# Latent attention and two window layers on one core: guard, turns from x, weight loads, paired values

## The chip, the cores and the metric

One NeuronCore of a Trainium2 chip runs the whole program. The metric is device time in microseconds (us), the median of the runs of one kernel. The engines are TensorE (PE; its weight loads PEld), VectorE (DVE), ScalarE (ACT), GpSimd (POOL) and SyncE (SP), which here only issues transfers. Each engine works through its own queue in order; semaphores tie them together.

## The reference

x has 4 sequences of 1024 tokens, 128 channels, float32.

```python
x = x + layernorm(latent_attention(layernorm(x)))      # 16 heads of 8, causal softmax over 1024 keys
x = x + layernorm(window_layers(layernorm(x)))         # 2 layers

# a window layer: 8 heads of 64, windows of 64 tokens, each sees itself and the one before
h = shift_token(x)                    # half of the channels from the token before
q, k, v = split(h @ wqkv)
q = q / clip(norm(q), 1e-12) * qs     # k the same
q, k = rotary_xpos(q, k)
x = x + local_attention(q, k, v) @ wo
h = layernorm(shift_token(x)) * lg + lb
a, g = split(h @ w1 + b1)
x = x + (a * gelu(g)) @ w2 + b2
```

## The kernel before, in words

The program is a row of stages; a block of instructions for each engine ends before the next begins. `project` makes the queries, keys and values of the latent attention; `attend` is the causal attention; `mix` multiplies with W_o, normalises and adds; then for each of two layers `window` and `mlp`; `last_norm` closes.

**attend** runs 16 stages (4 sequences x 4 groups of 4 heads). A stage has 12 score groups, called steps here (0 to 11): step n covers one half of the queries (steps 0 to 3 the first half, 4 to 11 the second) and one tile of 128 keys, for 4 heads; the widths are 512, 384, 256, 128 and 512 five times, 384, 256, 128 columns. For each step TensorE issues four scores (L444) into a ring of three banks, psE, and between them four "maxima units" of the next stage (L429, with the causal mask L432) into a ring of four banks, psM. ScalarE takes the exponential of each score (L514) into one of four `prob` buffers; VectorE takes the maximum of each unit (L593); GpSimd masks the diagonal tiles (L549). Behind the scores of step G TensorE issues `values(G - 2)`: four heads side by side as tiles of 128 rows by 32 columns of its array, float32, two passes each (L458, eight instructions), summed in one bank, psO. At a half's end ScalarE copies psO (L526, at steps 2 and 6) and the next first key tile's values wait for it; TensorE turns the copy (L478, behind the scores of steps 4 and 8). Maxima of the next stage are turned as 12-column transposes (L470) behind the scores of steps 0 and 5.

**mix** works on 8 chunks of 512 tokens. ScalarE first copies a chunk of `o_tok` into `oc` (L740), TensorE turns it (L719), ScalarE copies the turn (L736), TensorE multiplies with W_o (L726), then statistics, normalisation and residual go between VectorE, GpSimd and ScalarE.

**window** works on 32 tiles of 128 tokens per layer, in slots: in slot s tile s is projected (L904, L908), tile s-1 normalised, tile s-2 turned and scored, tile s-3 goes through softmax and values, tile s-4 through `wo`. The x of tile s+2 is turned for its projection (L897) near the end of the slot. SyncE first copies it from `xf` to a staging tile `xc` (L875), and spreads the values V of tile t over two buffers `vb` (L881, L882). The order of SyncE's queue is: x of tiles 0 and 1, the 14 loads of the MLP's weights (L660 to L673), then per slot x of tile s and V of tile s-2.

For the norms ScalarE squares, VectorE sums per head (L1135) and guards against zero with a tensor_scalar maximum (L1139), GpSimd raises to -0.5 (L1102, the `pow`). GpSimd's queue per slot is: `pow` of tile s-1, four sine products of tile s, called rotations here (L1092), and their addition to the cosine product (L1097). VectorE's queue per slot is: K copies (L1159, from PSUM, and L1162, within SBUF), reciprocal (L1179) and product (L1182) of the softmax, residual (L1186), cosine product (L1144), two maxima (L1169), carry (L1130), copy (L1174), the product with the norms (L1153, which waits for `pow` and for the addition), sums (L1135), guard (L1139). At a layer's start VectorE clears three tiles, scales the cosine and sine tables and then makes the first carries.

```python
dve.tensor_scalar(ssm[:, r % 2, :], ss[:, r % 2, :], 1e-24, None, ALU.max).then_inc(ssm_done, 1)      # L1139
ge(act, av_done, G - NPROB + 1)                                                                       # ScalarE, before the exponentials of step G
halves(sp, av_done, t, -4)                                                                            # SyncE, before V of tile t is spread
```

## Time and profile before

| | us |
|---|---|
| median of 3 runs | 1540.82 (1539.07 to 1544.87) |
| profiled execution | 1543.41 |
| its span, first to last instruction | 1541.6 |
| attend, first maximum to last score group | 80 to 609 |
| mix | 611 to 656 |
| window layer 1, from its first turn | 661 to 994 |
| window layer 2, from its first turn | 1089 to 1424 |
| last norm | 1515 to 1541.6 |

| engine | busy us | share of the span |
|---|---|---|
| PE | 1299.2 | 84% |
| DVE | 1211.1 | 79% |
| ACT | 946.1 | 61% |
| POOL | 766.6 | 50% |

An engine is busy while one of its instructions runs; an instruction that has begun and waits inside counts as busy. The shares are means over stages with different limits, so the stages are to be read one by one.

### The profile page before, as it was taken

The page shows a single profiled execution, that of the slowest core. Times are in us where ns is not written, and L with a number is a line of the kernel's source. Part 1 is how long each engine was busy: PE and PEld are TensorE (multiplying, and loading weights), DVE is VectorE, ACT ScalarE, POOL GpSimd, SP SyncE. Part 2 cuts the span into 40 slices and gives each one's busy share as a digit, 9 for nine tenths or more (in the row PEclk, how much of TensorE's full clock was granted, in tenths as well). Part 3 has the DMA queues.
Part 4 walks back from the last instruction along what each step waited for, and adds up shares of the span by engine and source line. Part 5 has one row for each costly group of instructions (what it writes and reads, how often), then busy time and mean ns, then how long its engine had stood idle before and what let it go on. Part 6 is the DMA issues. An engine that isn't in the chain of part 4 may idle for free. (4 is left out here: it accounts for less than half of the span.)

```text
span 1541.6 us, 30997 instructions
## 1 busy us (share of the span) xinstructions
PE 1299.2 (84%) x11013; PEld 741.1 (48%) x11013; DVE 1211.1 (79%) x2530; ACT 946.1 (61%) x2605; POOL 766.6 (50%) x742
## 2 busy tenths in 40 slices
PE   4389999999999997359999999699589999997892
PEld 2243444444444442326666666465266666665561
DVE  5576878787888770659999999666499999997667
ACT  4425776777677766747777777332377777775220
POOL 1001212221222121469999999310599999994102
PEclk9757999999999998679999999989799999999896
DMA  4412111111111101121111111000211111110001
GB/s 111 141 47 65 36 51 50 36 34 53 48 36 35 36 4 41 56 50 36 36 36 36 36 36 32 9 1 1 49 27 36 36 36 36 36 34 16 1 1 55
DMA packets 44272, 59.59 MB, mean 39 GB/s; under 512 B 8130, under 2 KB 31948, under 8 KB 41804
## 3 DMA queue, kind: packets, MB, share of 16 engines
q1 hardware_dynamic: 43544, 57.47, 13.8%
q8 instruction: 89, 1.46, 0.4%
q14 instruction: 63, 0.52, 0.1%
q10 hardware_dynamic: 576, 0.15, 0.0%
HBM read 26.67 MB, written 8.39 MB: 23 GB/s over the span
## 5 line engine op out<-in xcount | busy, mean ns | idle before, releaser
L593 DVE TENSOR_REDUCE a_nm<-a_psM 128x1 f32<-128x512 f32 (+3 forms) x768 | 375.1, 550 | 118.2 <-PE a_psM L429 65.8
L514 ACT ACTIVATE a_prob<-a_psE 128x512 f32<-128x512 f32 (+3 forms) x768 | 326.2, 491 | 161.7 <-PE a_psE L444 160.1
L1092 POOL TENSOR_TENSOR w_t<-w_raw,w_sin 128x256 f32<-128x256 f32 x256 | 264.1, 1060 | 49.6 <-ACT w_raw L1018 49.6
L429 PE MATMUL a_psM<-a_ks,a_qs 72*128 72x512 bf16 (+3 forms) x768 | 251.9, 346 | 18.3 <-PEq L76 18.1
L549 POOL TENSOR_SCALAR_AFFINE_SELECT a_prob<-a_prob 128x512 f32<-128x512 f32 x128 | 81.4, 637 | 371.9 <-ACT a_prob L514 371.9
L444 PE MATMUL a_psE<-a_qs,a_ks 84*128 84x512 bf16 (+3 forms) x768 | 253.2, 339 | 9.4 <-DMA a_qs<-a_nmT 5.8
L1041 ACT ACTIVATE w_prob<-w_psS,w_bias 128x128 f32<-128x128 f32 x512 | 181.4, 367 | 48.5 <-DVE w_bias L1169 48.4
L1102 POOL TENSOR_TENSOR w_rn<-w_ssm,mhalf 128x16 f32<-128x16 f32 x64 | 186.5, 2914 | 6.4
L458 PE MATMUL a_psO<-a_prob,v_all 128*32 128x512 f32 (+3 forms) x1536 | 170.1, 510 | 11.5 <-ACT a_oT L526 11.5
L444 PEld LDWEIGHTS a_psE<-a_qs,a_ks 84*128 84x128 bf16 x768 | 74.6, 99 | 188.5 <-ACT a_prob L514 118.2
L1097 POOL TENSOR_TENSOR w_rot<-w_t 128x1024 f32<-128x1024 f32 x64 | 152.1, 2376 | 8.8 <-issue 0.4
L904 PE MATMUL w_psQK<-w_wqkv,w_hT 128*128 128x512 f32 x256 | 132.4, 642 | 0.2 <-ACT w_raw L1018 0.2
L432 PE MATMUL a_psM<-mask_q,ident_b 128*128 128x128 bf16 x512 | 116.6, 229 | 0.0
L1041 ACT ACTIVATION_READ_ACCUMULATOR w_prob<-w_psS,w_bias 128x1 f32 x512 | 104.3, 204 | 0.0
L1048 ACT ACTIVATE w_pT<-w_psT 128x512 f32<-128x512 f32 x64 | 38.2, 597 | 106.8 <-PE w_psT L948 106.8
L429 PEld LDWEIGHTS a_psM<-a_ks,a_qs 72*128 72x128 bf16 x768 | 78.2, 102 | 49.2 <-issue 23.5
L1144 DVE TENSOR_TENSOR w_t<-w_raw,w_cos 128x1024 f32<-128x1024 f32 x64 | 78.0, 1218 | 28.8 <-ACT w_raw L1018 23.9
L1153 DVE TENSOR_TENSOR w_rot<-w_rot,w_rn 128x1024 f32<-128x1024 f32 x64 | 91.3, 1426 | 3.2 <-POOL w_rn L1102 1.5
L1169 DVE TENSOR_REDUCE w_bias<-w_psS 128x4 f32<-128x512 f32 x128 | 87.0, 680 | 3.1 <-PE w_psS L937 3.1
L1277 PE MATMUL f_psU<-f_hT,f_w 128*114 128x512 f32 (+1 forms) x192 | 88.0, 609 | 0.0
L1139 DVE TENSOR_SCALAR w_ssm<-w_ss 128x16 f32<-128x16 f32 x64 | 82.3, 1286 | 2.2
L963 PE MATMUL w_psO<-w_pT,w_vb 128*64 128x64 f32 x1024 | 57.9, 234 | 27.5 <-ACT w_pT L1048 15.5
(139 smaller groups left out, 2509.9 us busy)
## 6 DMA issues: line engine op xcount, KB each, us to landing
w_vb<-w_v SPq DMA_DIRECT2D x128, 128.0 KB, 2.3
a_qs<-q_parts SPq DMA_DIRECT2D x16, 576.0 KB
a_ks<-k_parts SPq DMA_DIRECT2D x16, 576.0 KB
w_xc<-xf_sb SPq DMA_DIRECT2D x64, 64.0 KB, 2.0
q_parts<-p_parts SPq DMA_DIRECT2D x24, 128.0 KB
k_parts<-p_parts SPq DMA_DIRECT2D x24, 128.0 KB
out_x<-l_y SPq DMA_DIRECT2D x8, 256.0 KB, 2.3
a_qs<-a_nmT SPq DMA_DIRECT2D x32, 48.0 KB
```

The source lines that it names most:

```text
L429: mm = pe.matmul(out, qs[0:ROWS, g, j, i * P:(i + 1) * P], ks[0:ROWS, g, j, 512 * kc:512 * kc + n], start=True, stop=not diag)
L432: mm = pe.matmul(out[:, n - P:n], sb["ident_b"], sb["mask_q"], start=False, stop=True)
L444: pe.matmul(psE[:, r % NRING, 0:w], ks[0:KROWS, g, j, kt * P:(kt + 1) * P], qs[0:KROWS, g, j, q0:q0 + w], start=True, stop=True).then_inc( ...
L458: mm = pe.matmul(psO[32 * j:32 * j + 32, q0:512], v_flat[:, col + j * VA:col + j * VA + 32], prob[G % NPROB][:, j, 0:512 - q0], start=(kt ...
L514: act.activation(prob[G % NPROB][:, j, 0:w], psE[:, r % NRING, 0:w], ACT.Exp, scale=SCALE0).then_inc(e_read, 1)
L593: dve.tensor_reduce(nm[:, s % 2, kc, i, j:j + 1], psM[:, r % MRING, 0:n], AX.X, ALU.max, negate=True).then_inc(m_read, 1)
L904: pe.matmul(psQK[:, w, :], hT[:, r % 2, 0:P], wqkv[:, bass.ds(layer * (3 * INNER) + w * INNER, INNER)], start=True, stop=True).then_inc(qk ...
L1041: i = act.activation(prob[:, p, w, c, :], psS[:, w, c * P:(c + 1) * P], ACT.Exp, bias=bias[:, p, n:n + 1], accum_out=den[:, p, n:n + 1])
L1092: i = pool.tensor_tensor(out[:, w, :, half, :], src[:, w, :, 1 - half, :], tab, ALU.mult)
L1097: pool.tensor_tensor(rot[:, r % 2, :], t1[:, :], t2[:, :], ALU.add).then_inc(rot_done, 1)
L1102: pool.tensor_tensor(rn[:, r % 2, :], ssm[:, r % 2, :], sb["mhalf"][:, 0:16], ALU.pow).then_inc(rn_done, 1)
L1153: dve.tensor_tensor(both, both, rn[:, p, :].unsqueeze(2).broadcast_to((P, 16, DH)), ALU.mult).then_inc(unit_done, 1)
```

## The change

Four edits. The guard becomes a reduction with maximum over pairs: `ss` gets a second element beside each sum, set once per layer to 1e-24. In the window layers TensorE turns x straight from `xf`, the copies through `xc` go, and the MLP's weights are loaded behind V of tile 7. In the mix TensorE turns straight from `o_tok`, and ScalarE's copy goes. In attend the values are issued behind the scores of odd steps only, two groups at once, with five `prob` buffers.

```diff
--- before.py
+++ after.py
@@ -367,7 +367,7 @@
         def sem(name):
             return ctx.enter_context(nc.semaphore(name))
 
-        NPROB, NRING, MRING = 4, 3, 4
+        NPROB, NRING, MRING = 5, 3, 4
         qs, ks, v_flat = sb["qs"], sb["ks"], sb["v_flat"]
         prob = [tile(f"a_prob{r}", [P, HG, 512]) for r in range(NPROB)]
         oT = tile("a_oT", [P, 2, 512])
@@ -496,8 +496,10 @@
                     for qc in range(2):
                         if o_turn_group(e, qc) == G:
                             turn_outputs(e, qc)
-                if G >= AV_LAG:
-                    values(G - AV_LAG)
+                if G % 2:
+                    for behind in (AV_LAG + 1, AV_LAG):
+                        if G >= behind:
+                            values(G - behind)
             for G in GROUPS[-AV_LAG:]:
                 values(G)
             turn_outputs(NSTAGE - 1, 1)
@@ -682,7 +684,6 @@
         def sem(name):
             return ctx.enter_context(nc.semaphore("m_" + name))
 
-        oc = tile("m_oc", [P, 2, 4, P])
         ocT = tile("m_ocT", [P, 2, 4, P])
         stats = tile("m_stats", [P, 2, 4, 4, 6])
         mv = tile("m_mv", [P, 2, 4, 4, 2])
@@ -693,7 +694,7 @@
         psT = ctx.enter_context(nc.psum_tensor("m_psT", [P, 2, 512], F32))
         psA = ctx.enter_context(nc.psum_tensor("m_psA", [P, 4, 512], F32))
 
-        w_in, o_staged, oT_done, oT_copied, a_done = sem("w_in"), sem("o_staged"), sem("oT_done"), sem("oT_copied"), sem("a_done")
+        w_in, oT_done, oT_copied, a_done = sem("w_in"), sem("oT_done"), sem("oT_copied"), sem("a_done")
         stats_done = [sem("stats_a"), sem("stats_x")]
         mean_done = [sem("mean_a"), sem("mean_x")]
         var_done = [sem("var_a"), sem("var_x")]
@@ -712,11 +713,10 @@
             pe.wait_ge(w_in, 16)
 
             def turn(c, r):
-                at_least(pe, o_staged, 0, c, 1)
                 at_least(pe, oT_copied, 0, c, -1)
                 p = r % 2
                 for t in range(4):
-                    i = pe.transpose(psT[:, p, t * P:(t + 1) * P], oc[:, p, t, :], sb["ident"])
+                    i = pe.transpose(psT[:, p, t * P:(t + 1) * P], sb["o_tok"][:, c * 4 + t, :], sb["ident"])
                 i.then_inc(oT_done, 1)
 
             def project_out(c, r):
@@ -735,10 +735,6 @@
                 at_least(act, a_done, 0, c, -1)
                 act.activation(ocT[:, r % 2, :, :].rearrange("p t c -> p (t c)"), psT[:, r % 2, :], ACT.Copy).then_inc(oT_copied, 1)
 
-            def stage(c, r):
-                at_least(act, oT_done, 0, c, -1)
-                act.activation(oc[:, r % 2, :, :], sb["o_tok"][:, bass.ts(c, 4), :], ACT.Copy).then_inc(o_staged, 1)
-
             def normal(w, c, p, outs, ins, done):
 
                 at_least(act, shift_done[w], 0, c, 1)
@@ -753,7 +749,7 @@
             def layers_input(c, r):
                 normal(1, c, r, lambda t: sb["xf"][:, c * 4 + t, :], lambda t: sb["x"][:, c * 4 + t, :], xf_done)
 
-            pipelined(act, NCH, 4, [(1, copy), (0, stage), (3, normal_a), (5, layers_input)])
+            pipelined(act, NCH, 4, [(1, copy), (3, normal_a), (5, layers_input)])
 
         @block.gpsimd
         def _(pool):
@@ -823,10 +819,9 @@
 
         wqkv, wo = sb["wqkv"], sb["wo"]
         cos, sin = tile("w_cos", [P, TB, 2, DH]), tile("w_sin", [P, TB, 2, DH])
-        xc = tile("w_xc", [P, 2, D])
         hT = tile("w_hT", [P, 2, P + 1])
         sq = tile("w_sq", [P, 2 * INNER])
-        ss, ssm, rn = tile("w_ss", [P, 2, 16]), tile("w_ssm", [P, 2, 16]), tile("w_rn", [P, 2, 16])
+        ss, ssm, rn = tile("w_ss", [P, 2, 16, 2]), tile("w_ssm", [P, 2, 16]), tile("w_rn", [P, 2, 16])
         raw = tile("w_raw", [P, 2, 2 * INNER])
         t1, t2 = tile("w_t1", [P, 2 * INNER]), tile("w_t2", [P, 2 * INNER])
         rot = tile("w_rot", [P, 2, 2 * INNER])
@@ -845,7 +840,6 @@
         psO = ctx.enter_context(nc.psum_tensor(f"w_psO_{layer}", [P, 512], F32))
 
         w_in, tables, zeroed = sb["w_in"], sem("tables"), sem("zeroed")
-        xc_in = [sem("xc_in0"), sem("xc_in1")]
         vb_in = [sem(f"vb_in{r}") for r in range(4)]
         xT_done, hT_copied, carried = sem("xT_done"), sem("hT_copied"), sem("carried")
         qk_done, v_done, sq_done, ss_done, ssm_done, rn_done = (sem(x) for x in ("qk_done", "v_done", "sq_done", "ss_done", "ssm_done", "rn_done"))
@@ -870,10 +864,6 @@
 
         @block.sync
         def _(sp):
-            def load_x(t, r):
-                at_least(sp, xT_done, base, t, -1)
-                sp.dma_start(xc[:, r % 2, :], sb["xf"][:, t, :]).then_inc(xc_in[r % 2], 16)
-
             def spread_v(t, r):
 
                 at_least(sp, v_copied, base, t, 1)
@@ -881,20 +871,18 @@
                 sp.dma_start(vb[r][0:WIN, :], v[r][0:WIN, :]).then_inc(vb_in[r], 16)
                 sp.dma_start(vb[(r + 1) % 4][WIN:P, :], v[r][WIN:P, :]).then_inc(vb_in[r], 16)
 
-            sp.wait_ge(zeroed, layer * 3 + 3)
-            for t in range(2):
-                load_x(t, t)
-            load_mlp_weights(nc, sp, io, sb, layer)
-            pipelined(sp, NT, 4, [(0, lambda t, r: None if isinstance(t, int) and t < 2 else load_x(t, r)), (2, spread_v)])
+            sp.wait_ge(zeroed, layer * 4 + 4)
+            for t in range(NT):
+                if t == 8:
+                    load_mlp_weights(nc, sp, io, sb, layer)
+                spread_v(t, t % 4)
 
         @block.tensor
         def _(pe):
             def turn_x(t, r):
-                p = r % 2
-                pe.wait_ge(xc_in[p], (base + t - p) * 8 + 16)
                 at_least(pe, pT_copied[0], base, t, -4)
                 at_least(pe, hT_copied, base, t, 0)
-                pe.transpose(psT[:, 0, 0:P], xc[:, p, :], sb["ident"]).then_inc(xT_done, 1)
+                pe.transpose(psT[:, 0, 0:P], sb["xf"][:, t, :], sb["ident"]).then_inc(xT_done, 1)
 
             def project_qk(t, r, w):
                 if w == 0:
@@ -1074,7 +1062,7 @@
                 if runs(s - 2):
                     exps(s - 2, r2, 1)
 
-            act.wait_ge(zeroed, layer * 3 + 3)
+            act.wait_ge(zeroed, layer * 4 + 4)
             copy_hT(0, 0)
             copy_hT(1, 1)
             slots(act, slot)
@@ -1110,6 +1098,7 @@
             dve.memset(hT[WIN:P, 1, P:P + 1], 0.0).then_inc(zeroed, 1)
             dve.memset(kT[:, 1, :, :], 0.0).then_inc(zeroed, 1)
             dve.memset(vb[0][WIN:P, :], 0.0).then_inc(zeroed, 1)
+            dve.memset(ss[:, :, :, 1], 1e-24).then_inc(zeroed, 1)
 
             dve.wait_ge(w_in, WINDOW_LOADS)
             for w in range(2):
@@ -1119,7 +1108,7 @@
                     sc = sb["scales"][:, bass.ds(layer, 1), w, 32 - 32 * half:64 - 32 * half].broadcast_to((P, TB, 32))
                     part = slice(32 * half, 32 * half + 32)
                     dve.tensor_tensor(sin[:, :, w, part], sb["sin"][:, :, w, part], sc, ALU.mult).then_inc(tables, 1)
-            dve.wait_ge(zeroed, layer * 3 + 3)
+            dve.wait_ge(zeroed, layer * 4 + 4)
             dve.wait_ge(tables, layer * 6 + 6)
 
             def carry(t, r):
@@ -1132,11 +1121,11 @@
 
             def sums(t, r):
                 at_least(dve, sq_done, base, t, 1)
-                dve.tensor_reduce(ss[:, r % 2, :], sq[:, :].rearrange("p (h d) -> p h d", d=DH), AX.X, ALU.add).then_inc(ss_done, 1)
+                dve.tensor_reduce(ss[:, r % 2, :, 0], sq[:, :].rearrange("p (h d) -> p h d", d=DH), AX.X, ALU.add).then_inc(ss_done, 1)
                 at_least(dve, ss_done, base, t, 1)
                 at_least(dve, rn_done, base, t, -1)
 
-                dve.tensor_scalar(ssm[:, r % 2, :], ss[:, r % 2, :], 1e-24, None, ALU.max).then_inc(ssm_done, 1)
+                dve.tensor_reduce(ssm[:, r % 2, :], ss[:, r % 2, :, :], AX.X, ALU.max).then_inc(ssm_done, 1)
 
             def cosines(t, r):
                 at_least(dve, raw_done, base, t, 1)
```

## Rows read from the trace of the kernel before

**Rows 1.** Stretches: us, busy PE, PEld, DVE, ACT, POOL (count), PE clock, DMA share, GB/s.
```profile
240.00:340.00 100.00, 97.44 (x798) 44.20 (x800) 80.06 (x174) 71.83 (x174) 22.19 (x51) 1.00 0.14 40
700.00:800.00 100.00, 91.39 (x990) 60.68 (x988) 98.33 (x134) 77.67 (x251) 97.32 (x63) 1.00 0.16 38
```

**Rows 2.** Timeline, attention, TensorE: start, us, what [idle before it].
```profile
301.21 0.22 PE L432 MATMUL a_psM<-mask_q,ident_b 128*128 128x128 bf16 x1
...
301.27 0.22 PE L444 MATMUL a_psE<-a_qs,a_ks 84*128 84x128 bf16 x1
...
301.89 0.22 PE L432 MATMUL a_psM<-mask_q,ident_b 128*128 128x128 bf16 x1
...
302.04 0.85 PE L458 MATMUL a_psO<-a_prob,v_all 128*32 128x384 f32 x8
...
302.83 0.39 PE L444 MATMUL a_psE<-a_qs,a_ks 84*128 84x512 bf16 x1
...
309.35 1.07 PE L458 MATMUL a_psO<-a_prob,v_all 128*32 128x512 f32 x8 [0.38 <-ACT a_oT L526]
...
310.35 0.23 PE L444 MATMUL a_psE<-a_qs,a_ks 84*128 84x128 bf16 x1
...
333.42 0.39 PE L444 MATMUL a_psE<-a_qs,a_ks 84*128 84x512 bf16 x1
```

**Rows 3.** Timeline, attention, ScalarE.
```profile
303.32 2.07 ACT L514 ACTIVATE a_prob<-a_psE 128x512 f32<-128x512 f32 x4 [1.06 <-PE a_psE L444]
...
308.06 0.66 ACT L514 ACTIVATE a_prob<-a_psE 128x256 f32<-128x256 f32 x2 [0.42 <-PE a_psE L444]
...
308.61 0.60 ACT L526 ACTIVATE a_oT<-a_psO 128x512 f32<-128x512 f32 x1
```

**Rows 4.** Timeline, window layer 1, one steady tile: VectorE and GpSimd.
```profile
780.28 2.91 POOL L1102 TENSOR_TENSOR w_rn<-w_ssm,mhalf 128x16 f32<-128x16 f32 x1
...
782.48 1.22 DVE L1144 TENSOR_TENSOR w_t<-w_raw,w_cos 128x1024 f32<-128x1024 f32 x1
...
783.15 4.16 POOL L1092 TENSOR_TENSOR w_t<-w_raw,w_sin 128x256 f32<-128x256 f32 x4
...
787.45 2.37 POOL L1097 TENSOR_TENSOR w_rot<-w_t 128x1024 f32<-128x1024 f32 x1
...
788.49 1.35 DVE L1139 TENSOR_SCALAR w_ssm<-w_ss 128x16 f32<-128x16 f32 x1
...
789.92 2.91 POOL L1102 TENSOR_TENSOR w_rn<-w_ssm,mhalf 128x16 f32<-128x16 f32 x1
...
790.36 0.28 DVE L1162 COPY w_kT<-w_kT 128x256 f32<-128x256 f32 x1
```

**Rows 5.** Timeline, window layer 1, an early tile: VectorE and GpSimd.
```profile
687.63 3.77 POOL L1092 TENSOR_TENSOR w_t<-w_raw,w_sin 128x256 f32<-128x256 f32 x4
...
691.21 0.22 DVE L1139 TENSOR_SCALAR w_ssm<-w_ss 128x16 f32<-128x16 f32 x1
...
691.53 2.35 POOL L1097 TENSOR_TENSOR w_rot<-w_t 128x1024 f32<-128x1024 f32 x1
...
692.11 1.92 DVE L1162 COPY w_kT<-w_kT 128x256 f32<-128x256 f32 x1
...
693.84 2.97 POOL L1102 TENSOR_TENSOR w_rn<-w_ssm,mhalf 128x16 f32<-128x16 f32 x1
```

**Rows 6.** Timeline, start of window layer 1.
```profile
660.57 0.58 SPq L660 DMA_DIRECT2D f_w<-in_w  x1
...
670.67 0.47 SPq L875 DMA_DIRECT2D w_xc<-xf_sb  x1
...
672.88 0.48 PE L897 MATMUL w_psT<-ident,w_xc 128*128 128x128 f32 x1 [5.94 <-DMA w_xc<-xf_sb]
...
677.50 1.76 POOL L1092 TENSOR_TENSOR w_t<-w_raw,w_sin 128x256 f32<-128x256 f32 x1 [1.13 <-ACT w_raw L1018]
```

**Rows 7.** Tile m_oc: count, ns minimum/median/maximum, first and last start.
```profile
L740 ACT ACTIVATE m_oc<-o_tok x8: 621/630/654, 610.8 to 635.8; 128x512 f32<-128x512 f32 x8
```

## The prediction, made before the result was known

> **What bounds the kernel now.** I read the profile in this order: the mean busy time of each engine by stretch, then one period of each of the two long loops in order of time, then the starts of the stages. The chain that ended last covers only the closing norm and says nothing of this change.
>
> The busy table [rows 1] shows two regimes. In the causal attention TensorE is busy 97.4 of 100 us at full clock, VectorE 80, ScalarE 72: TensorE's queue sets the pace. In the window layers VectorE (98.3) and GpSimd (97.3) are both full, TensorE 91.4, ScalarE 77.7. Two engines "full" together are suspicious: one of them may only be waiting inside its instructions. The attention's period, first score of step 0 to the same in the next stage, is 333.42 - 302.83 = 30.59 us [rows 2], 16 stages. The window's period, from one `pow` on GpSimd to the next, is 789.92 - 780.28 = 9.64 us [rows 4], 64 tiles in two layers.
>
> **Part 1, the guard as a maximum over pairs (L1139).** The tensor_scalar on 16 elements took 1.35 us in the steady loop, from 788.49 to 789.84; GpSimd's addition L1097 ran from 787.45 to 789.82 [rows 4]. For an early tile the same instruction came before the addition began and took 0.22 [rows 5]. So it does no work for 1.15 us: it waits for GpSimd to leave something the two share, and the next `pow`, which needs its result, starts at 789.92. The copy L1162 (SBUF to SBUF) shows the same: 1.92 us at 692.11, ending at 694.03, after the addition that ran from 691.53 to 693.88 [rows 5]. The new operation, a tensor_reduce over 16 pairs, is not in the trace. Bounds: 0.2 us (the unblocked 0.22) and 1.35 (it waits just the same). I take 0.2: the loop's other operations of this kind take no longer beside GpSimd, and this one has 32 elements. The Trainium skill (SBUF — State Buffer, Who interferes with whom) states that on this chip a tensor_reduce never contends with GpSimd, while a tensor_scalar or a copy in a two-port mode waits for a whole GpSimd instruction or makes it wait; the two rows at L1139 agree with the second half, and no row here shows the first for so small an operation.
>
> VectorE thus gets back 1.15 us of 9.64, to 8.5. It doesn't keep that: with the guard out of the way, K's copy L1159 and then L1162 come earlier, and L1162 meets the addition that the guard used to meet; about 0.35 us is waited there. VectorE needs 8.85. GpSimd becomes the bound. Its period now: 2.87 from `pow` to the first rotation, 4.30 for four rotations (783.15 to 787.45), 2.47 from the addition to the next `pow` [rows 4]. The first rotation starts at 783.15 while the two-input product L1144 still runs until 783.70. For the early tile the same pieces took 691.53 - 687.63 = 3.90 and 693.84 - 691.53 = 2.31 [rows 5]: with 2.87 a period of 9.08. What remains in it is the collision with L1153, which needs the `pow` and so always falls on a rotation. With VectorE about 0.5 us earlier at L1144, that product ends at about the first rotation; with the guard done long before, `pow` follows the addition directly. I take 9.2, between 9.08 and 9.64 and near the lower: 0.1 for what is left of L1144 and of L1162's turn. The gain is 0.44 us for some 55 tiles (64 less four or five at each layer's start), **24 us**, bounds 5 (only the gap in front of `pow`, 0.1 each) and 31 (9.08). Behind GpSimd stands TensorE, with 0.914 x 9.64 = 8.8 us of work per tile [rows 1] and a few tenths of handovers; that is late next. At each layer's end the last L1159 comes 0.5 us or more earlier: 1 us together.
>
> Against the full gain: L1162, queued behind the addition, may run ahead of `pow` and hold it for its own 0.28. In the trace they met once: the `pow` at 693.84, begun before L1162's end at 694.03, took 2.97 instead of 2.91 [rows 4, 5], so the row says 0.06. With 0.28 in place of 0.06 the period is 9.42; that is a rival below. The same section of the Trainium skill, by which the first holds the shared port pair for its whole instruction, would give that rival's 0.28; the row gives less.
>
> **Part 2, turns straight from x and later MLP weights.** After the first two copies SyncE issues 14 weight loads, from 660.57 to 670.67, in front of the third x copy; TensorE waits 5.94 us for it, until 672.88 [rows 6]. Without the copies that wait is gone. It isn't worth 5.94. GpSimd is busy with tile 0 all that time and idles only 1.13 us before tile 1's rotation at 677.50 [rows 6]. From there on it is full. So 1.1 us, and some 0.4 because the first turn no longer waits for a copy: the first projection waits for the hT carry behind VectorE's tables. Bounds 0 and 5.9 per layer; I take 1.5, nearest to GpSimd's idle time, **3 us** for two layers. The new memset puts under 0.2 us in front of the tables in each layer, -0.3.
>
> The 10.1 us of loads now stand in SyncE's queue in front of the V copies of tile 8, and the tiles behind. Those leave when tile 5's values are done and are read three tiles later, 27.6 us at 9.2 each. 10.1 of issue and a few us of landing fit with over 10 us to spare. Cost nothing; if the cover were gone, the excess in each layer. The x copies themselves leave the queue; nobody waited for them in the steady loop.
>
> **Part 3, no staging copy in the mix.** ScalarE loses eight copies of 0.63 [rows 7], 5.0 us of work. The mix is a chain of handovers between four engines at chunk pace, where ScalarE mostly waits; TensorE's turn of a chunk also has to wait for the previous chunk. Bounds 0 and 5; I take **1**, near the lower.
>
> **Part 4, values of two groups together.** L432 to L444 is 0.06 us (301.21, 301.27), L432 to the values' first pass 0.15 (301.89, 302.04): going to four tiles of 32 columns costs 0.09. A group of 384 columns lasts 0.79 until the next score, one of 512 columns 1.00 (309.35 to 310.35): 0.21 per 128 columns, hence 0.15 that isn't columns, of which I give 0.09 to going back and the rest to the stagger of the four tiles, which stays [rows 2]. Pairing saves both ways once per pair: 0.18. Of six pairs per stage one keeps its switch, because the maxima's 12-column transposes after step 0 no longer stand next to values: 5 x 0.18 = 0.9 us. Also, values of a first key tile wait for ScalarE's copy of the previous sums, 0.38 us at 309.35 [rows 2], twice a stage. In the new order a whole step of scores lies between: 0.8 more.
>
> Against it: eight scores in a row with a ring of three banks. The sixth score needs the third exponential. Exponentials of 512 columns go at 0.5 us each (2.07 for four), of 256 at 0.33, and the copy L526 of 0.60 stands after the second at steps 2 and 6 [rows 3]. At steps 2 and 3 the third exponential ends about 1.8 us after the first score, and the sixth score could go at 1.4: it waits 0.45, a later one 0.1. At steps 6 and 7 the same comes to 0.4, at 10 and 11 to 0.1; elsewhere the next bank is free just in time. Together 1.1 us per stage. VectorE's maxima (ring of four) keep up. Net 0.9 + 0.8 - 1.1 = 0.6 us, 16 stages, **10 us**; bounds 0 (the waits take it all) and 18 (half of the waits don't come). The last stage has no maxima units and is paced by ScalarE either way. The fifth buffer keeps the exponentials free: with it those of an odd step need values that TensorE issued behind the scores of two steps before, as now, and those of an even step one step more.
>
> **The sum.** 24 + 1 + 3 - 0.3 + 1 + 10 = 38.7 us. The profiled execution took 1543.4 (span 1541.6 and 1.8 around it), which makes 1504.7; it lies 2.6 over the median of 1540.8. Against the median: **1502 us**.
>
> **Rivals.**
> A. The waiting copy L1162 takes its turn in full and holds `pow`: period 9.42, gain 12 instead of 24, **1514**. For: that it waits at all in the early tile; against: the 0.06.
> B. The ring waits eat the attention's gain: **1512**. For: ScalarE's margins at steps 0, 1, 4, 5 are under 0.1 us by my count. Against: with every wait counted the total isn't above zero.
> C. The early start is worth its full wait and GpSimd reaches 9.08: 31 + 1 + 12 + 1 + 10 = 55, **1486**. For: TensorE stood idle 5.94; against: GpSimd didn't.
> D. The reduction waits for GpSimd as the guard did. The change then doesn't do what it says; 24 and 1 fall away: **1527**. Nothing in the trace speaks for it.
> E. Slower: VectorE gets so far ahead that the two-input product L1182, now under `pow`, falls on the addition L1097 and holds it. GpSimd then pays its 1.2 us per tile: 9.2 + 1.2 = 10.4, 55 x 0.76 = 42 more than now, less 14 of the rest: **1569**. It decides once L1162, which stands in front of L1182, reaches VectorE before the addition starts at 787.45, 2.9 us earlier than it runs now (790.36). Against: in a collision L1162 itself waits for the addition's end [rows 5], and its data come from TensorE late.
>
> **How the numbers follow.** Forecast 0.53, A 0.13, B 0.12, C 0.10, D 0.07, E 0.05. From 1485 to 1526 holds the forecast, A, B and most of C; the ends also take the bounds of parts 1 and 4 together (1502 - 7 - 8 and 1502 + 12 + 10). A measurement of this kernel can tell about 0.5% (8 us) from no change. Below 1533 lie the forecast and A to D, less a little where several fail together: faster 0.90. Same 0.05, slower 0.05 (E).
>
> **What would show it.** Period of `pow` near 9.2, the guard at 0.2, L1162 longer than 0.28 and ending with L1097; rotations of 3.9 together. Attention period near 30.0, no wait of the values for L526, new waits of L444 for L514 at steps 3 and 7. GpSimd's idle time before tile 1 gone. Wrong would be: a guard of 1 us or more, a `pow` much over 2.91, a TensorE wait for V copies around tile 11, or an attention period over 30.6.

## The result: 1492.6 us, and the profile after

The changed kernel takes 1492.63 us (median of 4 runs, 1491.60 to 1497.84), where the kernel before took 1541.78 in the same session (4 runs). The ratio is 0.9687, with a 95% interval from 0.9658 to 0.9717: 48 us less (44 to 53). The forecast was 39 less, 1502, in a range from 1485 to 1526.

The profiled execution of after took 1497.84, with a span of 1496.1, against 1543.41 and 1541.6 before. It is the slowest of its four, so where its stretches are compared below, 45.6 us are explained, not 48.

The mean busy times of the same two stretches as in [rows 1]: first the attention, then window layer 1. The columns are the same.

```profile
240.00:340.00 100.00, 98.60 (x804) 46.61 (x800) 81.33 (x177) 73.25 (x174) 20.42 (x49) 1.00 0.16 45
700.00:800.00 100.00, 96.23 (x1063) 64.00 (x1063) 97.88 (x144) 81.58 (x262) 98.54 (x66) 1.00 0.17 38
```

All that changed is density. GpSimd is at 98.54 and stays the bound of the window layers; TensorE, from 91.39 to 96.23, has come close behind. Its work per tile is the same as before: 0.9623 x 9.15 = 8.8 us, as 0.914 x 9.64 was. VectorE still reads 98, though the guard gave it back 1.16 us per tile. Of these the copy takes 0.41, where [rows 5] had hinted, and the product with the norms 0.19; the rest is the shorter period. The steady tile that answers to [rows 4] shows it. VectorE first (timeline of after):

```profile
785.78 0.19 DVE L1128 TENSOR_REDUCE w_ssm<-w_ss 128x16 f32<-128x32 f32 x1
785.94 0.69 DVE L1148 COPY w_kT<-w_psT 128x512 f32<-128x512 f32 x1
786.55 0.69 DVE L1151 COPY w_kT<-w_kT 128x256 f32<-128x256 f32 x1
787.16 0.19 DVE L1168 RECIPROCAL w_rden<-w_den 128x8 f32<-128x8 f32 x1
787.39 1.22 DVE L1171 TENSOR_TENSOR w_prob<-w_prob,w_rden 128x1024 f32<-128x1024 f32 x1
788.53 0.28 DVE L1175 TENSOR_TENSOR xf_sb<-xf_sb,w_psO 128x128 f32<-128x128 f32 x1
788.73 1.22 DVE L1133 TENSOR_TENSOR w_t<-w_raw,w_cos 128x1024 f32<-128x1024 f32 x1
...
791.55 1.62 DVE L1142 TENSOR_TENSOR w_rot<-w_rot,w_rn 128x1024 f32<-128x1024 f32 x1
```

and GpSimd over the same time:

```profile
784.73 2.36 POOL L1085 TENSOR_TENSOR w_rot<-w_t 128x1024 f32<-128x1024 f32 x1
787.04 2.97 POOL L1090 TENSOR_TENSOR w_rn<-w_ssm,mhalf 128x16 f32<-128x16 f32 x1
789.98 3.76 POOL L1080 TENSOR_TENSOR w_t<-w_raw,w_sin 128x256 f32<-128x256 f32 x4
793.88 2.37 POOL L1085 TENSOR_TENSOR w_rot<-w_t 128x1024 f32<-128x1024 f32 x1
796.20 2.96 POOL L1090 TENSOR_TENSOR w_rn<-w_ssm,mhalf 128x16 f32<-128x16 f32 x1
```

The guard (now L1128) takes 0.19 in the middle of the addition L1085. The copy L1151, which was L1162, takes 0.69 instead of 0.28: it starts at 786.55 inside the addition and ends at 787.24, just after the addition's end at 787.09. The product L1142, which was L1153, takes 1.62 instead of 1.43. `pow` takes 2.97 instead of 2.91. The period is 796.20 - 787.04 = 9.16 here and 9.15 on average, in three pieces: 2.94 from `pow` to the first rotation, 3.90 for the rotations, 2.32 from the addition to the next `pow`. Before they were 2.87, 4.30 and 2.47. The cosine product L1133 ends at 789.95, and the first rotation starts at 789.98: the overlap that had stretched the rotations to 4.16 busy us is gone.

In the attention, the timeline of TensorE shows the new order in a steady stage that answers to [rows 2]. Scores of step 3 and the values behind them, then the first two scores of step 7:

```profile
296.67 0.22 PE L444 MATMUL a_psE<-a_qs,a_ks 84*128 84x128 bf16 x1
296.90 0.39 PE L429 MATMUL a_psM<-a_ks,a_qs 72*128 72x512 bf16 x1
297.40 0.23 PE L444 MATMUL a_psE<-a_qs,a_ks 84*128 84x128 bf16 x1
...
298.09 0.22 PE L432 MATMUL a_psM<-mask_q,ident_b 128*128 128x128 bf16 x1
298.24 1.71 PE L458 MATMUL a_psO<-a_prob,v_all 128*32 128x512 f32 x16
299.88 0.39 PE L444 MATMUL a_psE<-a_qs,a_ks 84*128 84x512 bf16 x1
...
306.46 0.38 PE L444 MATMUL a_psE<-a_qs,a_ks 84*128 84x512 bf16 x1
306.68 0.38 PE L429 MATMUL a_psM<-a_ks,a_qs 72*128 72x512 bf16 x1
307.30 0.39 PE L444 MATMUL a_psE<-a_qs,a_ks 84*128 84x512 bf16 x1 [0.24 <-ACT a_prob L516]
```

Sixteen value instructions stand together, without a wait in front, and take 1.64 us until the next score. Before, one group of 512 columns and one of 384 took 1.00 + 0.79. The price is to be seen too: from the first score of step 3 to the second is 0.73 where the trace of before has 0.29, and from the first score of step 7 to the second 0.84 where it has 0.44. The groups of the page say the same of the whole kernel (columns: busy us, mean ns, idle before and its releaser):

```profile
L444 PE MATMUL a_psE<-a_qs,a_ks 84*128 84x512 bf16 (+3 forms) x768 | 251.9, 336 | 13.2 <-ACT a_prob L516 6.9
...
L458 PE MATMUL a_psO<-a_prob,v_all 128*32 128x512 f32 (+3 forms) x1536 | 148.1, 502 | 0.0
```

Before, L458 was busy for 170.1 and idle for 11.5 behind the copy L526; L444 was idle for 9.4.

Where the 45.6 us of the profiled executions went, from the first and last starts of each stage in the two traces (two single executions; how far the stages vary from one to another is said with the experiments):

| | before | after | difference |
|---|---|---|---|
| attention, first maximum to last values | 527.8 | 507.9 | -19.9 |
| of it stage 0, first score to the next stage's | 53.33 | 44.34 | -9.0 |
| of it each steady stage | 30.59 | 29.74 | -0.85 |
| mix, first turn to last residual | 44.3 | 45.7 | +1.4 |
| window layer 1, last residual to the MLP's first product | 338.5 | 326.0 | -12.5 |
| window layer 2, the same | 341.9 | 325.4 | -16.5 |
| all the rest | | | +1.9 |

### The profile page after: what moved, and what is told of

It reads as the page before. It is cut to its first block and busy times, and to the rows that moved or that the text cites. A ratio compares the mean times of both kernels' runs of the same rounds, so it can differ in the third digit from the quotient of the medians.

```text
span 1496.1 us, 30910 instructions
## 1 busy us (share of the span) xinstructions
PE 1294.6 (87%) x11013; PEld 757.0 (51%) x11013; DVE 1180.9 (79%) x2532; ACT 934.8 (62%) x2597; POOL 742.3 (50%) x742
## 5 line engine op out<-in xcount | busy, mean ns | idle before, releaser
L516 ACT ACTIVATE a_prob<-a_psE 128x512 f32<-128x512 f32 (+3 forms) x768 | 319.4, 499 | 147.9 <-PE a_psE L444 146.1
L444 PE MATMUL a_psE<-a_qs,a_ks 84*128 84x512 bf16 (+3 forms) x768 | 251.9, 336 | 13.2 <-ACT a_prob L516 6.9
L1080 POOL TENSOR_TENSOR w_t<-w_raw,w_sin 128x256 f32<-128x256 f32 x256 | 239.9, 966 | 47.2 <-ACT w_raw L1006 47.2
L1085 POOL TENSOR_TENSOR w_rot<-w_t 128x1024 f32<-128x1024 f32 x64 | 152.0, 2374 | 8.8 <-issue 0.4
L458 PE MATMUL a_psO<-a_prob,v_all 128*32 128x512 f32 (+3 forms) x1536 | 148.1, 502 | 0.0
L444 PEld LDWEIGHTS a_psE<-a_qs,a_ks 84*128 84x128 bf16 x768 | 74.9, 98 | 142.7 <-issue 49.3
L1142 DVE TENSOR_TENSOR w_rot<-w_rot,w_rn 128x1024 f32<-128x1024 f32 x64 | 103.1, 1611 | 4.4 <-POOL w_rn L1090 2.7
L1133 DVE TENSOR_TENSOR w_t<-w_raw,w_cos 128x1024 f32<-128x1024 f32 x64 | 78.0, 1219 | 16.8 <-ACT w_raw L1006 9.7
L904 PEld LDWEIGHTS w_psT<-ident,w_rot 128*128 128x128 f32 x512 | 60.6, 143 | 48.3 <-issue 29.0
L904 PE MATMUL w_psT<-ident,w_rot 128*128 128x128 f32 x512 | 68.5, 278 | 14.7 <-DVE w_rot L1142 14.6
```

Of the source, the lines that this page charges most:

```text
L444: pe.matmul(psE[:, r % NRING, 0:w], ks[0:KROWS, g, j, kt * P:(kt + 1) * P], qs[0:KROWS, g, j, q0:q0 + w], start=True, stop=True).then_inc( ...
L458: mm = pe.matmul(psO[32 * j:32 * j + 32, q0:512], v_flat[:, col + j * VA:col + j * VA + 32], prob[G % NPROB][:, j, 0:512 - q0], start=(kt ...
L516: act.activation(prob[G % NPROB][:, j, 0:w], psE[:, r % NRING, 0:w], ACT.Exp, scale=SCALE0).then_inc(e_read, 1)
L904: i = pe.transpose(psT[:, w, c * P:(c + 1) * P], rot[:, r % 2, w * INNER + c * P:w * INNER + (c + 1) * P], sb["ident"])
L1080: i = pool.tensor_tensor(out[:, w, :, half, :], src[:, w, :, 1 - half, :], tab, ALU.mult)
L1085: pool.tensor_tensor(rot[:, r % 2, :], t1[:, :], t2[:, :], ALU.add).then_inc(rot_done, 1)
```

## The experiments: each part alone

**The guard alone** (e1_guard).

```
-  ss = tile("w_ss", [P, 2, 16])
+  ss = tile("w_ss", [P, 2, 16, 2])      # second of each pair set to 1e-24
-  dve.tensor_scalar(ssm[:, r % 2, :], ss[:, r % 2, :], 1e-24, None, ALU.max)
+  dve.tensor_reduce(ssm[:, r % 2, :], ss[:, r % 2, :, :], AX.X, ALU.max)
```

> Before with the new guard alone. Forecast's theory (the tensor_scalar waited for GpSimd's addition and held up pow): the window period falls from 9.64 to about 9.15 as in after, the guard takes 0.19, the copy L1162 gets longer; 25 to 28 us less in all (ratio 0.982 to 0.984). Rival (most of the window gain comes from SyncE's queue without x copies): the period stays above 9.4, less than 14 us.

Measured: 1515.49 against 1542.77, ratio 0.9831 (0.9806 to 0.9855), 26 us less (22 to 30). The tile `w_ssm` in its trace (count, ns minimum/median/maximum):

```profile
L1140 DVE TENSOR_REDUCE w_ssm<-w_ss x64: 185/186/189, 665.4 to 1367.9; 128x16 f32<-128x32 f32 x64
L1102 POOL TENSOR_TENSOR w_rn<-w_ssm,mhalf x64: 2909/2960/2974, 668.9 to 1369.8; 128x16 f32<-128x16 f32 x64
```

All 64 reductions lie within 4 ns, and 58 of them begin while GpSimd's addition runs. The period is 9.15 with this edit alone, and the two window layers together are 27 us shorter than in the trace of before. The guard is more than half of the change.

**Turns from x and later weight loads alone** (e2_turns).

```
-  for t in range(2): load_x(t, t)
-  load_mlp_weights(...)
-  pipelined(sp, NT, 4, [(0, load_x), (2, spread_v)])
+  for t in range(NT):
+      if t == 8: load_mlp_weights(...)
+      spread_v(t, t % 4)
-  pe.transpose(psT[:, 0, 0:P], xc[:, p, :], sb["ident"])
+  pe.transpose(psT[:, 0, 0:P], sb["xf"][:, t, :], sb["ident"])
```

> Before with turns straight from x and the later weight loads alone. Forecast's theory: period stays 9.64, only GpSimd's idle time at the starts goes, 3 to 4 us in all (ratio 0.997 to 0.998). Rival: TensorE's wait for the third x copy is worth its whole length in each layer, 12 us (0.992). Second rival: V copies late behind the weight loads, a wait of TensorE for them near tile 11 and a longer layer.

Measured: 1539.57, ratio 0.9969 (0.9949 to 0.9989), 4.8 us less (1.7 to 7.9). The period stays at 9.64. So x copies and the order of SyncE's queue are nothing to the steady loop. What is left are the two starts: the second `pow` follows the last residual 2.1 us earlier in layer 1 and 2.8 in layer 2 than in the trace of before, together the size of the gain. (The whole layers can't show it, since a layer's length scatters by up to 4 us between traces.)

**Paired values and five buffers alone** (e3_pairs).

```
-  if G >= AV_LAG: values(G - AV_LAG)
+  if G % 2:
+      for behind in (AV_LAG + 1, AV_LAG):
+          if G >= behind: values(G - behind)
-  NPROB, NRING, MRING = 4, 3, 4
+  NPROB, NRING, MRING = 5, 3, 4
```

> Before with paired values and five buffers alone. Theory: period of a stage 29.74 instead of 30.59 in the fourteen steady stages, 12 us; and in stage 0 TensorE's clock is granted earlier than before (in after by about 20 us of time), another 7 to 9 us; 20 us in all (ratio 0.987). Rival: the early clock in stage 0 is chance of one execution and has nothing to do with the order: then stage 0 stays at 53 us and the gain is 11 to 13 us (0.992).

Measured: 1528.94, ratio 0.9921 (0.9896 to 0.9945), 12 us less (8 to 16), median of 9 runs that lie far apart (1524.01 to 1538.96). Every steady stage takes 29.74, as in after. The profiled execution is the fastest of the nine, 1524.01, and has a stage 0 of 44.21 us. That is the trace that the expectation's theory foresaw, but 12 us is the total that its rival foresaw: about 14 x 0.85, the steady stages without stage 0. The slowest run also had the lowest mean clock of TensorE, 0.918, against 0.932 in the profiled one. Whether the slower eight kept their clock in stage 0, no run shows.

**No staging copy in the mix alone** (e4_mix).

```
-  act.activation(oc[:, r % 2, :, :], sb["o_tok"][:, bass.ts(c, 4), :], ACT.Copy)
-  pe.transpose(psT[:, p, t * P:(t + 1) * P], oc[:, p, t, :], sb["ident"])
+  pe.transpose(psT[:, p, t * P:(t + 1) * P], sb["o_tok"][:, c * 4 + t, :], sb["ident"])
```

> Before without the mix's staging copy alone. Forecast: 1 us less. Rival from the profile of after (mix 1.4 us longer there): no gain or a loss of 1 to 2 us, since ScalarE's copies stood in time in which it waited, and TensorE's clock falls differently. Both lie within what can be told in total time; the mix's length in the trace decides, from the first turn to the last xf (44.3 us in before, 45.7 in after).

Measured: 1543.19, ratio 1.0004 (0.9985 to 1.0024): no change. The groups of its page show where ScalarE's 5.1 us went:

```profile
L724 PE MATMUL m_psA<-w_o,m_ocT 128*128 128x128 f32 x64 | 14.5, 399 | 11.2 <-ACT m_ocT L734 11.2
...
L734 ACT ACTIVATE m_ocT<-m_psT 128x512 f32<-128x512 f32 x8 | 4.8, 594 | 10.3 <-PE m_psT L717 10.3
```

ScalarE waits 10.3 us for TensorE's turns where it waited 6.0 with the copy in its queue; TensorE's own wait for ScalarE went from 12.2 to 11.2 only. The mix's length, which was to decide, is 45.0 us here. The traces that keep the copy (before, e1, e2, e3, e5, e6, e7, e12) have 43.1 to 46.5, so neither a gain nor a loss is shown, and the 1.4 us by which after's mix is longer in the table above lie within that scatter.

**Guard and pairs together** (e12_guard_and_pairs), the two edits above on the kernel before.

> Before with the guard and the paired values, without the turns from x, the later loads and the mix's edit. If the parts only add up, 27.3 + 13.8 = 41 us less (ratio 0.973), and after lies 3 to 8 us below; if the turns are worth more beside the faster guard (GpSimd less full at the starts), after lies over 8 us below.

Measured: 1503.21, ratio 0.9716 (0.9683 to 0.9749), where after has 0.9687 (0.9658 to 0.9717). The four single parts add up to 1.69 + 0.31 + 0.79 - 0.04 = 2.75%, where after saves 3.13% (2.83 to 3.42). With intervals of a quarter of a per cent on each part that is no contradiction; neither does it show that they add up exactly. After lies 0.29% or 4.5 us under this run, by the ratios, so the first of the two expectations came, though the intervals of the two ratios overlap. Against e1, the pairs are worth 1.15% or 18 us here (about 12 to 24), where alone on the kernel before they were worth 12. The profiled execution again was the fastest of its four (1494.44), and again the others had lower clocks (0.922 to 0.928 against 0.932).

## The experiments: why the guard no longer waits

Is it the pairs' layout, or the operation? Two kernels keep the pairs and change only the operation that reads them.

**A tensor_scalar over the first of each pair** (e5_guard_strided).

```
-  dve.tensor_reduce(ssm[:, r % 2, :], ss[:, r % 2, :, :], AX.X, ALU.max)
+  dve.tensor_scalar(ssm[:, r % 2, :], ss[:, r % 2, :, 0], 1e-24, None, ALU.max)
```

> Before with the pairs' layout of the sums (every second element), but the guard still a tensor_scalar that reads them at a stride of two. Theory A: any tensor_scalar waits for GpSimd's addition: guard 1.35 us, window period 9.64. Theory B: only one over contiguous float32 waits, since only that reads its source in a way that needs what GpSimd uses: guard about 0.2, period about 9.15 as with the reduction.

**A maximum of the two halves as two inputs** (e6_guard_two_inputs).

```
+  dve.tensor_tensor(ssm[:, r % 2, :], ss[:, r % 2, :, 0], ss[:, r % 2, :, 1], ALU.max)
```

> Before with the guard as a tensor_tensor maximum of the two elements of each pair, two sources in SBUF. If what is fought over is a second read path that two-source operations use (as L1153 and L1144 suggest, which hold up the rotations), it waits for the addition like the old guard: 1.3 us, period 9.64. Rival: VectorE's small operations are free of it unless they are tensor_scalar or copies: 0.2 and 9.15.

Measured: 1542.70 and 1548.12, against 1547.16 for the kernel before in the same session. Tile `w_ssm` in the trace of e5, and below it in that of e6:

```profile
L1140 DVE TENSOR_SCALAR w_ssm<-w_ss x64: 175/1347/2033, 667.2 to 1398.4; 128x16 f32<-128x16 f32 x64
```

```profile
L1140 DVE TENSOR_TENSOR w_ssm<-w_ss x64: 174/1349/2041, 669.1 to 1405.7; 128x16 f32<-128x16 f32 x64
```

Both wait just as the guard of before did, 1.35 us at the median and 0.17 when nothing stands in the way, and the period stays at 9.64 and 9.65. Stride doesn't help, nor does a plain two-input operation. Of the three forms tried, all 16 results wide, only the reduction goes past the addition. The Trainium skill (SBUF — State Buffer, Who interferes with whom) names just this split: on this chip a tensor_reduce never contends, a two-input operation does against a GpSimd instruction that reads. The three rows agree. One pair of rows doesn't: L1171 has two inputs in SBUF and runs under `pow`, which reads two tiles, in 1.22 us as everywhere else in the trace, so against that instruction the rule doesn't hold here. The cause of the guard's wait, something that VectorE and GpSimd share, is read from where the waits end; which part of the chip it is, no run here shows.

## The experiments: the attention's rings and buffers

**A bank from the maxima's ring to the scores'** (e8_after_rings), the sum of the two kept.

```
-  NPROB, NRING, MRING = 5, 3, 4
+  NPROB, NRING, MRING = 5, 4, 3
```

> After with four score banks and three banks for maxima instead of three and four. Theory of the forecast (the paired order pays about 1 us per stage because the sixth to eighth score wait for a bank): those waits at steps 3 and 7 go, period of a stage 28.9 to 29.2 instead of 29.74 if the maxima can do with three banks, 8 to 12 us less. Rival: VectorE's maxima are slower per unit (0.6 us at 512 columns) than TensorE's issue, and with three banks TensorE waits for them: period over 29.74, slower.

Measured: 1505.45, ratio 0.9739 (0.9698 to 0.9780), so 8 us more than after by the ratios; a steady stage takes 30.68 instead of 29.74, so the expectation's rival came; the last stage, without maxima, gives some of it back. The waits of TensorE's weight loads, which see a wait that hides under a product still running (us in total, times, longest), in e8:

```profile
PEld a_psM L429 <- DVE a_nm L595: 75.5, 214, 0.7
...
PEld a_psE L444 <- ACT a_prob L516: 28.7, 69, 0.9
```

and in after:

```profile
PEld a_psE L444 <- ACT a_prob L516: 48.2, 139, 0.9
...
PEld a_psM L429 <- DVE a_nm L595: 9.0, 37, 0.5
```

The fourth score bank does take waits away, 48.2 down to 28.7, and steps 6 and 7 together are 0.29 us shorter (5.70 against 5.99). But the maxima with three banks wait 75.5 instead of 9.0, and steps 2 and 3 are 0.48 longer, 4 and 5 0.18, 8 and 9 0.60. So the ring waits of the new order are real, and with 3 + 4 + 1 banks in use for scores, maxima and values, moving one of them only moves the waits.

**Four buffers in place of five** (e11_after_4_buffers).

```
-  NPROB, NRING, MRING = 5, 3, 4
+  NPROB, NRING, MRING = 4, 3, 4
```

> After with four prob buffers instead of five. By TensorE's order the values that free a buffer are issued before the scores whose exponentials need it, for even and for odd steps, so the period stays 29.74 or grows by under 0.2 us per stage. Rival: the fifth buffer carries the paired order, since an even step's exponential now waits for the last values of the pair in front: 0.5 us or more per stage.

Measured: 1492.84 in one run, stages of 29.74. The fifth buffer isn't needed. ScalarE waits for scores almost all the time it waits at all; the room it might gain in `prob` it can't use.

## The experiments: where the 9 us of stage 0 come from

Stage 0 is 9 us shorter in after than in before, and nothing in the prediction spoke of it. The stretches of before (busy PE, PEld, DVE, ACT, POOL, PE clock, DMA share, GB/s):

```profile
115.00:120.00 5.00, 2.44 (x22) 1.13 (x22) 2.72 (x7) 1.57 (x3) 1.45 (x5) 0.94 0.32 74
120.00:125.00 5.00, 5.00 (x23) 1.89 (x22) 3.47 (x9) 1.99 (x5) 0.00 (x0) 0.50 0.77 177
...
135.00:140.00 5.00, 5.00 (x19) 1.36 (x18) 2.50 (x4) 2.34 (x4) 0.00 (x0) 0.51 0.19 77
140.00:145.00 5.00, 5.00 (x36) 2.25 (x38) 4.18 (x9) 3.47 (x8) 0.64 (x1) 1.00 0.01 5
```

and of after:

```profile
115.00:120.00 5.00, 4.54 (x31) 1.93 (x29) 1.44 (x3) 1.28 (x3) 1.45 (x5) 0.69 0.27 56
120.00:125.00 5.00, 4.77 (x28) 1.79 (x26) 5.00 (x13) 3.99 (x7) 0.00 (x0) 1.00 0.75 179
...
135.00:140.00 5.00, 5.00 (x47) 2.41 (x45) 4.67 (x14) 3.10 (x11) 2.17 (x7) 1.00 0.19 79
```

Before, TensorE came up to 2.4 GHz after 112 us, stood idle from 116, fell back to 1.2 and stayed there for some 20 us, busy all the time: 18 to 26 instructions in 5 us instead of 28 to 47. In after it never stood idle for long, and came up only at 118. All the traces fall in two groups (us; the clock is the granted one):

| traces | stage 0 | clock comes up | falls back | up again |
|---|---|---|---|---|
| before | 53.33 | 113 | 120 | 140 |
| e1, e2, e4, e5, e6, the old order too | 50.19 to 51.25 | 110 to 114 | 117 to 121 | 134 to 136 |
| after, e3, e8 to e12, the new order | 44.21 to 46.37 | 117 to 120 | never in stage 0 | |

So the clock's fall belongs to the old order in every trace, and before's 53.33 is the longest stage 0 of its kind: 6 to 7 us is the usual difference to after's 44.34, and 9 is that of the two executions compared. The instruction at which the two differ is the first score of step 4, which waits for the transfer of the turned maxima. In before (timeline of TensorE):

```profile
118.53 0.39 PE L444 MATMUL a_psE<-a_qs,a_ks 84*128 84x512 bf16 x1 [2.56 <-DMA a_qs<-a_nmT]
```

and in after, where the values of two groups stand in front of it:

```profile
115.47 2.95 PE L458 MATMUL a_psO<-a_prob,v_all 128*32 128x512 f32 x13
118.88 0.39 PE L444 MATMUL a_psE<-a_qs,a_ks 84*128 84x512 bf16 x1 [0.46 <-DMA a_qs<-a_nmT]
```

The transfer lands 0.35 us apart in the two. The two differ in more than the idle time, since in after the clock was still at half while the values ran. Is it the idle stretch that costs the clock?

**The kernel before with that wait filled** (e7_before_filled): ten products of scores that the next score overwrites, in front of the wait. They add work of no use. The wait for a free bank moves ahead of the one for the transfer; the rest of the kernel is as it was.

```
+  ge(pe, e_read, r - NRING + 1)
+  if G == 4 and j == 0:
+      for _ in range(10):
+          pe.matmul(psE[...], ks[...], qs[...], start=True, stop=True)
   if kt == 0 and j == 0: pe.wait_ge(nm_in[qc], 16 * e + 16)
-  ge(pe, e_read, r - NRING + 1)
```

> Before, with ten extra matrix products of 512 columns on TensorE in stage 0 in front of its wait for the transfer of the second half's maxima (step 4), their result overwritten. Theory (the clock falls because TensorE idles there 3.3 us, and stays at half for 20 us more): granted clock 1.0 from about 120 us on, stage 0 of 44 to 46 us instead of 50 to 53, 5 to 8 us less in all. Rival: the clock's fall has another cause (or comes from its own rhythm): stage 0 stays at 50 or more, or gets longer by the 2 to 4 us that the extra products take.

Measured: 1536.53, ratio 0.9950 (0.9928 to 0.9973), 7.7 us less (4.2 to 11.1), with more work. The timeline and the stretches of its trace:

```profile
115.78 2.33 PE L444 MATMUL a_psE<-a_qs,a_ks 72*128 72x512 bf16 x10
118.39 0.39 PE L447 MATMUL a_psE<-a_qs,a_ks 84*128 84x512 bf16 x1 [0.28 <-DMA a_qs<-a_nmT]
```

```profile
115.00:120.00 5.00, 4.71 (x32) 1.83 (x30) 2.73 (x6) 1.69 (x4) 1.44 (x5) 1.00 0.35 79
120.00:125.00 5.00, 4.88 (x43) 2.17 (x42) 5.00 (x12) 3.54 (x7) 0.00 (x0) 1.00 0.74 170
```

The clock came up at 112 us, as in the other traces of the old order, and it holds. (The expectation's 3.3 us of idle time is that of the weight loads, 3.25; the products' own is 2.56.) Stage 0 takes 44.54 us, where the six traces without the filling take 50.19 to 53.33, and the attention 519.2, where before, e1, e2 and e4 take 523.0 to 527.8. So in the old order the idle stretch before the transfer costs the clock, and the clock the time. The pairing avoids it by accident: it puts two groups of values in front of that wait, and runs them before the clock is up. Which of the two matters in the new order isn't separated.

**A clock held up before the attention** (e9_after_warm): stage 0 starts at half clock in before and after, behind some 18 us without work for TensorE. Eighteen float32 products without use stand at the end of the projection.

```
   pipelined(pe, NCH, 2, [(2, transposes), (3, heads)])
+  for _ in range(18): pe.matmul(psC[...], ident, ident x 4, start=True, stop=True)
```

> After, with 18 extra float32 products of 512 columns at the end of TensorE's queue in the projection stage (their bank is read by nobody), in the 18 us in which it waits for the stage's end. Theory (the clock is at half from 80 to 118 us because TensorE was idle before): the clock is 1.0 from 80 us on, the first scores and stage 0 come sooner; bound by VectorE's maxima then, 6 to 12 us less than after. Rival: the clock falls anyway in the attention's ramp, where TensorE waits for VectorE and for transfers: no gain beyond 2 us.

Measured: 1493.49, ratio 0.9643 (0.9607 to 0.9678), and stage 0 44.65 us, against 44.34. Its stretches:

```profile
80.00:85.00 5.00, 4.41 (x31) 1.73 (x30) 3.97 (x12) 0.00 (x0) 0.00 (x0) 1.00 0.33 128
85.00:90.00 5.00, 3.79 (x17) 1.43 (x16) 5.00 (x12) 0.00 (x0) 0.86 (x4) 0.79 0.21 84
90.00:95.00 5.00, 3.71 (x16) 1.52 (x15) 4.39 (x10) 0.59 (x1) 0.00 (x0) 0.50 0.04 18
...
115.00:120.00 5.00, 4.78 (x28) 1.67 (x20) 1.37 (x4) 1.69 (x4) 1.44 (x5) 0.64 0.32 80
```

The products keep full clock up to 85 us, and then it is lost all the same: at full clock TensorE is through its first maxima early and waits for VectorE, which is busy for 5.00 of 5. The waits are four, of 0.2 to 0.3 us each, between 86 and 89 us, and the clock falls at 88. That they are the cause is read from the trace alone. It comes back up at the same time as in after. The two ratios' intervals overlap (0.9607 to 0.9678, and 0.9658 to 0.9717), and the stage is no shorter: nothing won, as the rival said.

**Both fillings** (e10_after_warm_filled), e9 with the ten products of e7.

> The same, and also the ten overwritten products in front of the wait for the transfer at step 4 of stage 0. If that idle time would let the clock fall again, this one is 3 to 8 us better than the one without; if the clock holds either way, 0 to 2 us worse.

Measured: 1494.22, ratio 0.9649 (0.9624 to 0.9674). The clock is at 0.54 of full already in 80 to 85 us, at 0.50 up to 115, and full from 120 on: the same picture as after, with a stage 0 of 46.37 us, 1.7 longer than in e9. The ten products begin at 117.4, behind two groups of values that fill most of the wait already, and end after 2.6 us, past the 118.9 at which after's score begins. So they have hardly a wait to fill here, and this run doesn't test what they did in e7; of its two expectations, 0 to 2 us worse came. So there is no version here that beats the changed kernel beyond the measurement.

## Why the prediction was right, step by step

The time fell in the range, 9.4 us under the point. It lies nearer to rival C's 1486 than to the forecast's 1502, so the time alone wouldn't decide between them; the traces and the single edits do. The terms of the guard, the turns and the mix lie within what their edits measured alone. The pairs' term was too small in the steady stages, and the pairs brought something more that wasn't foreseen.

**The guard, 24 + 1 forecast, 26 measured alone** (22 to 30). The step that decided, 0.2 us for the reduction, measured 0.19. What followed from it came too: L1162 (now L1151) comes earlier and waits about 0.4 in the addition (0.35 forecast), the cosine product ends where the first rotation begins, `pow` follows the addition directly. The period of 9.15 was put at 9.2, between 9.08 and 9.64. The 0.07 over the lower end is one thing: `pow` takes 2.97 and not 2.91 when it meets the copy, in every steady tile. The 56 tiles at 9.64 in the trace of before (55 were used) times 0.49 give 27.4. VectorE needs 0.979 x 9.15 = 8.96 us per tile, forecast 8.85. The difference is the product L1142: in after it begins 0.20 into the third rotation (791.55 and 791.35), where L1153 in before began 0.37 into it, so it waits longer for that rotation's end. The forecast held this collision to be unchanged.

**Turns and weights, 3 - 0.3 forecast, 4.8 measured alone** (1.7 to 7.9). The wait of 5.94 us [rows 6] was indeed not worth 5.94. At the start of window layer 1 the first projection now waits for the carry behind the tables (timeline of TensorE in after):

```profile
640.19 0.45 PE L885 MATMUL w_psT<-ident,xf_sb 128*128 128x128 f32 x1 [14.36 <-PEq L680]
642.64 0.48 PE L885 MATMUL w_psT<-ident,xf_sb 128*128 128x128 f32 x1 [2.00 <-ACT w_hT L1000]
645.33 3.75 PE L892 MATMUL w_psQK<-w_wqkv,w_hT 128*128 128x512 f32 x4 [2.21 <-DVE w_hT L1119]
```

From the last residual of the mix to the second `pow` it is 26.2 us in after, 27.9 before; at the second layer, from the MLP's last, 26.8 against 29.5. In the trace of after the `pow` of the fourth tile then waits 3.1 us, once, with TensorE's clock at 0.50 from 675 to 680. That isn't the edit's doing: layer 2 of e6 and e7, which have the old turns, shows the same wait. The loads cost nothing in the queue: no row of TensorE's waits in after names a transfer in the window layers.

**The mix, 1 forecast, nothing measured** (from 2 us less to 4 more). The lower bound was the right one. ScalarE's copy stood in time that ScalarE waits out anyway.

**The pairs, 0.6 us a stage forecast, 0.85 measured.** The three terms can be read apart, by pairs of steps. The waits for the copy L526 were 0.7 a stage (0.8 forecast, from doubling the 0.38; the second of a stage is 0.34), and are gone. The ring waits, from the distances of the scores above what is usual, are 0.56 at steps 2 and 3, 0.50 at 6 and 7, 0.10 at 10 and 11: 1.16, forecast 1.1. So the switches must give 0.85 - 0.7 + 1.16 = 1.3, forecast 0.9. That is the term that was mis-sized. Of the 0.15 us by which a group of values is longer than its columns (0.16 by the rows, 0.79 - 3 x 0.21), I gave 0.09 to the way back to scores and let 0.06 stay as the stagger of the four tiles. It doesn't stay: two groups in a row, 512 and 384 columns, take 1.64 and not 1.79, the whole 0.15 less, and the 0.09 ahead comes on top. Steps 4 and 5, and 8 and 9, where nothing waits, are each 0.25 shorter (4.81 after 5.06, 5.91 after 6.16), and that is the price of one pairing: 0.24, not 0.18.

**What was not foreseen** is the clock of stage 0: 9 us between the two profiled executions, 6 to 7 against the other traces of the old order, and 7.7 in the times of e7. The sum had no term for it. The 2.56 us of idle time and the half clock behind it stood in the trace of before, in a stretch that the argument never looked at because it read only steady stages. For a change in the order of TensorE's instructions, a prologue at half clock is a stretch of its own.

**The rivals.** A (`pow` held for 0.28): the copy does meet `pow` in every tile, and the price is 0.06. B (the ring waits eat the gain): the waits are there at their size, the gain is larger. C: GpSimd came near 9.08, but the early start wasn't worth its wait (4.8 us in e2, where C had 12). That the time lies close to C's is chance, since C had no stage 0 in it either; without the 6 to 9 us there the time would be 1499 to 1502. D: no, 0.19. E: L1171 runs from 787.39 on, under `pow`, and never reaches the addition.

**What stays open.** The single runs of e3 and e12 scatter over 15 and 13 us, with lower clocks in the slower ones, and the 24 of before over 12 us. So how often an execution keeps its clock in stage 0 isn't known; the profiled ones with the new order did. Nor is it known why the pairs are worth 12 us alone and about 18 beside the guard. Every trace has a stretch at half clock in the first tiles of a window layer; why only three of them (layer 1 of after, layer 2 of e6 and e7) have the wait of 3.1 us wasn't tried.

## What to carry to other kernels

Where two engines share something and both read as full, find the smallest instruction whose time is out of all proportion to its size, and ask which form of the same operation doesn't take part; a guard of 16 elements was worth 26 us. Removing the wait moves the collision to the next instruction of that kind, so cost that one too. And before an idle stretch of TensorE is written off as harmless, look at the granted clock behind it: 2.6 us without work cost about 8 (4 to 11).

## What the runs showed of the hardware

- A tensor_reduce of 32 elements took 0.185 to 0.189 us in all 64 tiles of e1, 58 of them begun under GpSimd's addition; a tensor_scalar, contiguous or with stride, and a two-input maximum of the same size took 1.35 at the median.
- The two-input products L1171 and L1133, of 1024 columns, run under `pow` (2.97 us) in 1.22, as they did before. Yet the product L1142 takes 1.62: it begins at 791.55, inside the third rotation (791.35 to 792.08), and the fourth rotation, begun at 792.04, takes 1.70 instead of 0.72 and ends after the product (793.74 and 793.16). That reads as each waiting for the end of the one in front. So two inputs wait for an addition of 1024 columns (the small guard of e6) and for a product of 256, but not for a `pow` of 16.
- A switch of TensorE between score products and four tiles of 32 columns costs about 0.24 us there and back, an estimate: steps 4 and 5, and 8 and 9, each with one switch less and no other wait, are 0.25 shorter.
- At 1.2 GHz from 120 to 140 us, TensorE reads as busy for 5.00 of 5 us, with half the instructions. A busy share says nothing of the clock; the count beside it does.
